# Gram matrices of a four-layer GNN kernel built from a symmetric W^T W: half the blocks on the high side, a one-sided product, and the transpose added by the tensor engine

## The chip, the core and the metric

The kernel runs on one core of one Trainium2 chip. The metric is the device time of one execution in microseconds, as the median over runs. The core has a tensor engine (PE, matmuls; its weight loads are shown as PEld), a vector engine (DVE), a scalar engine (ACT), GpSimd (POOL) and a sync engine (SP) that issues the DMAs. Each engine works through its own queue in order and waits on semaphores for the others.

## The reference, cut to what matters

Four graph layers follow each other on x of 32 batches x 256 nodes x 512 features, each with a residual and a layer norm. Layers 1 and 3 hold the Gram matrices:

```python
z_l = jnp.einsum('bnd,ed->bne', h, W_lang)
z_g = jnp.einsum('bnd,ed->bne', h, W_grav)
zn = z_l / jnp.maximum(jnp.linalg.norm(z_l, axis=-1, keepdims=True), EPS)
A_l = jnp.maximum(jnp.einsum('bnd,bmd->bnm', zn, zn), 0.0) * not_eye
sq = jnp.sum(z_g * z_g, axis=-1, keepdims=True)
d2 = jnp.maximum(sq + jnp.swapaxes(sq, -1, -2) - 2.0 * jnp.einsum('bnd,bmd->bnm', z_g, z_g), 0.0)
A_g = jnp.exp(-d2 / (2.0 * sigma * sigma)) * not_eye
...
out = jnp.einsum('bnm,bmd->bnd', K, v)
return jnp.einsum('bnd,ed->bne', out, W_O)
```

So each of the two layers needs, per batch, the two 256 x 256 matrices G = H^T (W^T W) H for W = W_lang and W = W_grav, where H is the layer's input, features by nodes. From G come the norms (its diagonal), the cosines and the distances. Layer 0 is an attention over features with a 256 x 256 mixing matrix, and layer 2 is a product with a fixed 256 x 256 matrix.

## The kernel before

Every value that goes through a matmul is held as a high part (the value rounded by ACT to the matmul's 32-bit format) and a low part (the rest, by DVE), and a product is the sum of three: high x high, high x low, low x high. DVE's subtraction for a low part is always line L809, ACT's rounding is L592.

The batches run in two streams, s = 0 and s = 1, with buffers of their own. The order of the work on each engine is written out by hand as a sequence of *slots*. In each slot one stream does the projections, Gram matrices and values of one layer (1 or 3), while the other stream's remaining steps are put between them. A turn takes two batches (one of each stream) through all layers in four slots: middle, middle, seam, seam. There are 16 turns, 15 of them in full in a loop, and a start ahead of them in which the weights are prepared.

- A **middle slot** mixes in, for the other stream: norm_rows (the transposed norms, L311), transpose_k, mix_values (out = K v), layer2, and transpose_x (the next layer's input turned around).
- A **seam slot** mixes in the end of layer 3 of one batch of the other stream and layer 0 of its next batch: adj_x, k_rows, aggregate (L371, L375), softmax_sums (L384), sum_rows, transpose_x.

The steps of the slot's own stream, on PE, are: `project` (z = W h, 48 matmuls of 128x256 for each of W_lang and W_grav: L419 and L420 with the high part of h, L425 with its low part), `gram` (G = z^T z, 24 matmuls of 128x256 for each of the two, L441) and `values` (v, 24 matmuls of 128x512, L303 and L307). L303 and L307 are the helper `product`, L311 is the helper `flip`, a transpose on PE of a 128 x 128 block.

On DVE, `split_z` takes the low part of z. `squares_l` (L964) and `gauss_start` (L979) read the diagonals of the two Gram matrices, `norm_squares` (L988) writes the norms out as a matrix whose transposes norm_rows makes, and `cosine_start` is L972. `kernel_rows` and `kernel_mix` (L997 to L1022) build K. `scale_agg` is L935 and `normalise` L879; L1031 is add_kv, L1042 add_bias2, L927 and L928 sum_squares. POOL does an inverse square root for each norm (L1203, L1207), one split per batch (L1190) and the attention sums (L1199).

In the start, `prepare` flips the weights W_lang, W_grav and W_O block by block and splits them into high and low; the products W_O W_V ("vo") are made by matmuls. The eight weight matrices go through two staging buffers, so a load waits until the buffer has been read.

Of the kernel before, what the change touches and what calls it, by code (L numbers as in the profile page):

```python
# [43 lines left out]
def gnn_stack(nc, x, adj, wq, wk, bm, w1l, w1g, w1v, w1o, gate1, sigma1, bias2,  # L44
# [9 lines left out]
    with ctx:  # L54
# [86 lines left out]
        def squares(row):  # L141
# [39 lines left out]
        gram_done = sems("gram_done")  # L181
        v_done = sems("v_done")
# [31 lines left out]
        wv_rounded = sem("wv_rounded")  # L214
        wv_split = sem("wv_split")
# [8 lines left out]
        jobs = [("l", 0), ("o", 0), ("vo", 0), ("g", 0), ("l", 1), ("o", 1), ("vo", 1), ("g", 1)]  # L224
        nat_a, nat_b = full[1][:, 0:4, :], full[1][:, 4:8, :]
        nat = {"l": nat_a, "o": nat_a, "g": nat_b}

        loads = [(w1l, nat_a, None, 0), (w1v, nat_b, None, 0), (w1o, nat_a, prep_pe, 4), (w1g, nat_b, wv_split, 2),
                 (w3l, nat_a, prep_pe, 8), (w3v, nat_b, prep_pe, 16), (w3o, nat_a, prep_pe, 20),
                 (w3g, nat_b, wv_split, 4)]  # L230
        load_of_job = {0: 0, 1: 2, 3: 3, 4: 4, 5: 6, 7: 7}
        load_of_wv = (1, 5)
        wv_hi, wv_lo = XS[1], VS[1]
        hi_of = {(k, l): w_hi[l][k] for l in range(2) for k in names}
        lo_of = {(k, l): w_lo[l][k] for l in range(2) for k in names}
        for l in range(2):
            hi_of["o", l], lo_of["o", l] = ZS[1][:, 0:4, :], ZS[1][:, 4:8, :]
        adj_nat = full[0][:, 2, :].rearrange("p (t m) -> p t m", m=nodes)
# [8 lines left out]
        def _(sp):  # L247
# [30 lines left out]
            sp.wait_ge(prep_pe, 24)  # L278
# [14 lines left out]
        def _(pe):  # L293
# [28 lines left out]
            def prepare(q):  # L322
                kind, l = jobs[q]
                if kind == "vo":
                    pe.wait_ge(prep_out, 4 * q)
                    pe.wait_ge(wv_split, 2 * l + 2)
                else:
                    pe.wait_ge(w_loaded[load_of_job[q]], 16)
                for t in range(FT):
                    dst = psum[1][:, t, :]  # L330
                    if q:
                        pe.wait_ge(prep_out, 4 * (q - 1) + t + 1)
                    elif t == 3:
                        pe.wait_ge(adj_prep, 1)
                    cols = slice(t * P, (t + 1) * P)
                    if kind == "vo":
                        last = product(dst, [(wv_hi[:, e, cols], wv_lo[:, e, cols],
                                              hi_of["o", l][:, e, :], lo_of["o", l][:, e, :]) for e in range(FT)])
                    else:
                        for e in range(FT):  # L340
                            last = flip(dst[:, e * P:(e + 1) * P], nat[kind][:, e, cols])
                    last.then_inc(prep_pe, 1)

# [64 lines left out]
            def project(s, j, l, kind, e):  # L408

                bank = (3, 0, 1, 2)[2 * kind + e // 2]  # L410
                dst = psum[s][:, bank, (e % 2) * nodes:(e % 2 + 1) * nodes]
                wh, wl = w_hi[l]["lg"[kind]], w_lo[l]["lg"[kind]]
                cols = slice(e * P, (e + 1) * P)
                first = kind == 0 and e == 0
                for h in range(2):
                    if first:
                        pe.wait_ge(hth_ready[s], j * 4 + (2 * l + h + 1))
                    for d in (2 * h, 2 * h + 1):
                        mm(dst, wh[:, d, cols], HTH[s][:, d, :], start=(d == 0), stop=False)  # L419
                        mm(dst, wl[:, d, cols], HTH[s][:, d, :], start=False, stop=False)  # L420
                for h in range(2):
                    if first:
                        pe.wait_ge(htl_ready[s], j * 4 + (2 * l + h + 1))
                    for d in (2 * h, 2 * h + 1):
                        last = mm(dst, wh[:, d, cols], HTL[s][:, d, :], start=False, stop=(d == FT - 1))  # L425
                if e % 2:
                    last.then_inc(z_done[s], 1)

            def gram(s, j, l, kind, n):

                if n == 0:
                    pe.wait_ge(zl_ready[s], j * 8 + (4 * l + 2 * kind + 1))
                    pe.wait_ge(zh_ready[s], j * 8 + (4 * l + 2 * kind + 2))
                zh, zl = ZH[s][kind], ZL[s][kind]
                cols = slice(n * P, (n + 1) * P)
                hi = [(zh[:, e, cols], zh[:, e, :]) for e in range(FT)]
                lo = [p for e in range(FT) for p in ((zh[:, e, cols], zl[:, e, :]), (zl[:, e, cols], zh[:, e, :]))]
                for i, (a, b) in enumerate(hi + lo):
                    if n == 0 and i == len(hi):
                        pe.wait_ge(zl_ready[s], j * 8 + (4 * l + 2 * kind + 2))  # L440
                    last = mm(psum[s][:, (3, 1)[kind], n * nodes:(n + 1) * nodes], a, b,  # L441
                              start=(i == 0), stop=(i == 3 * FT - 1))
                if n == NT - 1:
                    last.then_inc(gram_done[s], 1)

            def values(s, j, l, n):

                cols = slice(n * P, (n + 1) * P)
                wh, wl = w_hi[l]["vo"], w_lo[l]["vo"]
                product(psum[s][:, 2 * n, :],  # L450
                        [(HTH[s][:, d, cols], HTL[s][:, d, cols], wh[:, d, :], wl[:, d, :])
                         for d in range(FT)]).then_inc(v_done[s], 1)
# [43 lines left out]
            def start():  # L496

                prepare(0)
                pe.wait_ge(adj_prep, 1)
                adj_x(0, 0)  # L500
                prepare(1)
                k_rows(0, 0)
                prepare(2)
                prepare(3)
                prepare(4)
                aggregate(0, 0, (0, 1, 2, 3))
                prepare(5)
                softmax_sums(0, 0)
                sum_rows(0, 0)
                prepare(6)  # L510
                prepare(7)
                transpose_x(0, 0, 0)

            def middle_slot(s, js, l, r, jr):

                norm_rows(r, jr, 0)
                for e in range(FT):
                    project(s, js, l, 0, e)
                transpose_k(r, jr, 0)
                project(s, js, l, 1, 0)  # L520
                mix_values(r, jr, 0)
                for e in range(1, FT):
                    project(s, js, l, 1, e)
                gram(s, js, l, 0, 0)
                gram(s, js, l, 0, 1)
                layer2(r, jr)
                gram(s, js, l, 1, 0)
                gram(s, js, l, 1, 1)
                values(s, js, l, 0)
                transpose_x(r, jr, 1)  # L530
                values(s, js, l, 1)

            def seam_slot(s, js, l, r, jr, jn):
# [3 lines left out]
                for e in range(3):  # L537
                    project(s, js, l, 0, e)
# [4 lines left out]
                project(s, js, l, 0, 3)  # L543
                project(s, js, l, 1, 0)
# [4 lines left out]
                project(s, js, l, 1, 1)  # L549
                if jr is not None:  # L550
                    mix_values(r, jr, 1, jn)
                project(s, js, l, 1, 2)
                project(s, js, l, 1, 3)
                if jn is not None:
                    aggregate(r, jn, (0, 1), jr)
                gram(s, js, l, 0, 0)
# [3 lines left out]
                gram(s, js, l, 0, 1)  # L560
                if jn is not None:
                    sum_rows(r, jn)
                gram(s, js, l, 1, 0)
                gram(s, js, l, 1, 1)
                values(s, js, l, 0)
                values(s, js, l, 1)
# [23 lines left out]
        def _(act):  # L590
# [3 lines left out]

            def prepare(q, tiles=range(FT)):
                for t in tiles:
                    act.wait_ge(prep_pe, 4 * q + t + 1)
                    run(hi_of[jobs[q]][:, t, :], psum[1][:, t, :]).then_inc(prep_hi, 1)

            def round_wv(l):  # L600
                act.wait_ge(w_loaded[load_of_wv[l]], 16)
                for h in range(2):
                    run(wv_hi[:, 2 * h:2 * h + 2, :], nat_b[:, 2 * h:2 * h + 2, :]).then_inc(wv_rounded, 1)
# [66 lines left out]

            def split_v(s, j, l, n):
# [39 lines left out]
            def start():  # L711
                split_x(0, 0)
                prepare(0)
                round_wv(0)
                split_adj_x(0, 0)
                prepare(1)
                gates()
                softmax_columns(0, 0)
                attention_start(0, 0)
                prepare(2, (0, 1))  # L720
                attention_end(0, 0)
                prepare(2, (2, 3))
                prepare(3)
                prepare(4)
                round_wv(1)
                prepare(5)
                sum_row(0, 0)
                relu_rows(0, 0)
                prepare(6)
# [3 lines left out]
            def middle_slot(s, js, l, r, jr):  # L733
# [3 lines left out]
                split_z(s, js, l, 0, 1)  # L737
                split_kt(r, jr, 0)
                split_z(s, js, l, 1, 0)
                split_x2(r, jr)  # L740
                split_z(s, js, l, 1, 1)
# [4 lines left out]
            def seam_slot(s, js, l, r, jr, jn):  # L746
# [9 lines left out]
                split_z(s, js, l, 0, 1)  # L756
                if jn is not None:
                    softmax_columns(r, jn)
# [4 lines left out]
                split_z(s, js, l, 1, 0)  # L763
                if jn is not None:
                    attention_end(r, jn)
                split_z(s, js, l, 1, 1)
# [28 lines left out]
        def _(dve):  # L795
# [53 lines left out]
            def prepare(q, tiles=range(FT)):  # L849
# [421 lines left out]
```

## Time and profile before

| | us |
|---|---|
| median of 3 runs | 2265.52 (2262.24 to 2265.63) |
| the profiled execution: its own time | 2265.96 |
| the profiled execution: span, first to last instruction | 2264.2 |
| PE busy in the span | 2230.2 (98%) |
| DVE busy | 1814.6 (80%) |
| ACT busy | 811.3 (36%) |
| POOL busy | 376.7 (17%) |
| one full turn of four slots | 136.8 |

A time of the device is about 1.8 us above the span of the same execution. The busy share of an engine is an average over slots with different limits; which wait ends last in a slot has to be read from the timeline of that slot. Slot boundaries are told by norm_rows, the first four flips of a slot.

### The profile page before, as it was taken

Reading aid. Unit: us, or ns where it says so; the run is one execution under the profiler, and the core shown is the slowest. Engines: PE = TensorE matmul, PEld = TensorE weight load, DVE = VectorE, ACT = ScalarE, POOL = GpSimd, SP = SyncE. Lnnn points to the kernel's source line nnn. Section 1 sums busy time; section 2 is a strip of 40 time slices with the busy share of each in tenths; the row PEclk is TensorE's granted clock in tenths of the full one; section 3 lists DMA queues with packets and bytes.
Section 4 is the critical chain, followed back from the end, with each engine's and each line's share of the span. In section 5 each row is a group of like instructions: output and inputs, shape, how many; then the busy total and the mean of one; then the engine's idle time right before and its main releaser. Section 6 shows DMA issues by size and latency. Waiting matters only on the chain.

```text
span 2264.2 us, 37798 instructions
## 1 busy us (share of the span) xinstructions
PE 2230.2 (98%) x15204; PEld 2046.7 (90%) x15204; DVE 1814.6 (80%) x4601; ACT 811.3 (36%) x1513; POOL 376.7 (17%) x326
## 2 busy tenths in 40 slices
PE   7999999999999999999999999999999999999997
PEld 5899999989999899999989999899999999999896
DVE  7678788787887878878787887878888787887875
ACT  5424234242433424333242333424334242342421
POOL 1102121120211202112120211202112021211200
PEclk9999999999999999999999999999999999999998
DMA  5000000000000100000000000100001000000000
GB/s 177 19 1 11 29 10 29 1 29 10 10 29 1 38 1 10 29 10 29 1 10 29 10 29 1 38 1 10 29 1 38 1 11 29 10 29 1 20 1 19
DMA packets 23664, 44.89 MB, mean 20 GB/s; under 512 B 2625, under 2 KB 2881, under 8 KB 23489
## 3 DMA queue, kind: packets, MB, share of 16 engines
q1 hardware_dynamic: 23488, 42.48, 5.6%
q8 instruction: 120, 1.97, 0.4%
q14 instruction: 56, 0.45, 0.1%
HBM read 25.70 MB, written 16.78 MB: 19 GB/s over the span
## 4 chain that ended last, share of the span: by engine, by line
PE 84%; DVE 12%; issue 3%; ACT 1%; DMA 0%; POOL 0%; SPq 0%; POOLq 0%; DVEq 0%; ACTq 0%
PE psum L303 20%; PE psum L441 14%; PE psum L307 10%; PE psum L425 10%; PE psum L419 10%; PE psum L420 9%; PE psum L311 6%; DVE zs L809 5%; DVE full L917 2%; PE psum L375 2%; DVE stats L865 2%; PE psum L371 1%; PE psum L384 1%; ACT vs L592 1%; DVE full L1031 1%
## 5 line engine op out<-in xcount | busy, mean ns | idle before, releaser
L441 PE MATMUL psum<-zs 128*128 128x256 f32 x3072 | 398.6, 285 | 0.0
L441 PEld LDWEIGHTS psum<-zs 128*128 128x128 f32 x3072 | 382.8, 192 | 4.9
L592 ACT ACTIVATE zs<-psum 128x512 fp32r<-128x512 f32 (+1 forms) x456 | 238.7, 532 | 397.0 <-PE psum L425 305.6
L1203 POOL TENSOR_TENSOR rstd<-veps,minus_half 128x2 f32<-128x2 f32 x128 | 102.2, 798 | 1207.9 <-DVE veps L874 1207.9
L809 DVE TENSOR_TENSOR zs<-psum,zs 128x512 fp32r<-128x512 f32 (+1 forms) x456 | 266.9, 610 | 23.5 <-ACT zs L592 21.7
L592 ACT ACTIVATE vs<-psum 128x512 fp32r<-128x512 f32 x128 | 76.5, 598 | 553.8 <-PE psum L307 553.8
L1199 POOL TENSOR_TENSOR full<-full 128x512 f32<-128x512 f32 x96 | 145.5, 1516 | 442.3 <-DVE zs L809 433.8
L311 PE MATMUL psum<-ident,full 128*128 128x128 f32 x1412 | 191.6, 276 | 19.1 <-DVE full L1022 5.2
L311 PEld LDWEIGHTS psum<-ident,full 128*128 128x128 f32 x1412 | 165.0, 142 | 34.6 <-DVE full L1022 5.5
L865 DVE BATCH_NORM_STATS2 stats<-full 128x6 f32<-128x512 f32 x256 | 163.5, 681 | 0.0
L1031 DVE SCALAR_TENSOR_TENSOR full<-psum,rdeg,full 128x512 f32<-128x512 f32 x128 | 96.0, 750 | 82.6 <-PE psum L307 82.6
L879 DVE TENSOR_SCALAR full<-full,mv,rstd 128x512 f32<-128x512 f32 x256 | 128.1, 542 | 35.0 <-POOL rstd L1203 35.0
L809 DVE TENSOR_TENSOR zs<-full,vs 128x512 fp32r<-128x512 f32 x128 | 148.9, 1203 | 1.3
L303 PE MATMUL psum<-vs,zs 128*128 128x512 f32 x512 | 139.6, 394 | 0.7 <-ACT zs L592 0.7
L371 PE MATMUL psum<-vs,zs 128*128 128x512 f32 x512 | 139.3, 394 | 0.8 <-ACT vs L592 0.8
L419 PE MATMUL psum<-xs,w0l_hi 128*128 128x256 f32 x512 | 131.6, 290 | 0.3 <-ACT xs L592 0.3
L419 PE MATMUL psum<-xs,w1g_hi 128*128 128x256 f32 x512 | 130.6, 288 | 0.0
L419 PE MATMUL psum<-xs,w1l_hi 128*128 128x256 f32 x512 | 130.6, 288 | 0.0
L419 PE MATMUL psum<-xs,w0g_hi 128*128 128x256 f32 x512 | 130.6, 288 | 0.0
L809 DVE TENSOR_TENSOR vs<-psum,vs 128x512 fp32r<-128x512 f32 x128 | 87.9, 687 | 52.3 <-ACT vs L592 52.3
L303 PE MATMUL psum<-w0vo_hi,xs 128*128 128x512 f32 x512 | 129.4, 395 | 0.0
L303 PE MATMUL psum<-w1vo_hi,xs 128*128 128x512 f32 x512 | 128.9, 394 | 0.0
(139 smaller groups left out, 5097.1 us busy)
## 6 DMA issues: line engine op xcount, KB each, us to landing
full<-in_x_dram SPq DMA_DIRECT2D x32, 512.0 KB, 4.1
out_dram<-full SPq DMA_DIRECT2D x32, 512.0 KB, 2.9
full<-in_L_gnn_W_lang_dram SPq DMA_DIRECT2D x2, 1024.0 KB, 6.2
full<-in_L_gnn_W_V_dram SPq DMA_DIRECT2D x2, 1024.0 KB, 7.1
full<-in_L_gnn_W_O_dram SPq DMA_DIRECT2D x2, 1024.0 KB, 6.6
full<-in_L_gnn_W_grav_dram SPq DMA_DIRECT2D x2, 1024.0 KB, 5.7
full<-in_adj_dram SPq DMA_DIRECT2D x1, 256.0 KB, 2.6
bias_row<-in_L_gnn_bias_dram SPq DMA_DIRECT2D x1, 256.0 KB, 6.9
```

The source lines that it names most:

```text
L303: mm(dst, a, b, start=(n == 0), stop=False)
L307: ins = mm(dst, a, b, start=False, stop=(n == len(last) - 1))
L311: return mm(dst, src, ident[:], is_transpose=True, start=True, stop=True)
L371: mm(psum[s][:, bank, :], y[s][:, t, o * P:(o + 1) * P], ATH[s][t], start=(t == 0 and y is YTH), stop=False)
L419: mm(dst, wh[:, d, cols], HTH[s][:, d, :], start=(d == 0), stop=False)
L420: mm(dst, wl[:, d, cols], HTH[s][:, d, :], start=False, stop=False)
L425: last = mm(dst, wh[:, d, cols], HTL[s][:, d, :], start=False, stop=(d == FT - 1))
L441: last = mm(psum[s][:, (3, 1)[kind], n * nodes:(n + 1) * nodes], a, b, start=(i == 0), stop=(i == 3 * FT - 1))
L592: return nc.scalar.activation(dst, src, func, **kw)
L809: return tt(dst, src, plain(hi), ALU.subtract)
L865: ins = nc.vector.bn_stats(stats[s][:, n, :], CUR[s][:, n, :])
L1199: nc.gpsimd.tensor_tensor(ATT[s][0], ATT[s][0], ATT[s][t], ALU.add).then_inc(att_sum[s], 1)
```

## The change

The Gram matrix is built from S = W^T W. In the start, S is made once for each of the four matrices: the weight is split as it lies (no flips), and `prepare` multiplies it with itself, only the blocks on and above the diagonal (widths 512, 384, 256 and 128). `mirror` flips these blocks for the part below. The low buffer of S holds the low parts on and above the diagonal; its diagonal blocks are low parts of *half* the block, and the high parts of the halved diagonal blocks lie in the unused part below.

In a slot, `project_hi` multiplies the high part of h with the upper triangle T of S alone (diagonal halved, S = T + T^T), so 20 matmuls for each kind instead of 32; `project_lo` multiplies the low part of h with the whole high part of S (16, as before). `gram` multiplies the result, high and low, with the high part of h: 16 matmuls for each kind instead of 24. ACT copies this half Gram matrix to memory (`copy_gram`), and `symmetrise` flips it on PE in four blocks that are added to the same bank. `values` is cut into head and tail, which are put at different places. DVE's readers of the diagonals now wait for `sym_done`. All other work is the same, except for its order.

```diff
-        jobs = [("l", 0), ("o", 0), ("vo", 0), ("g", 0), ("l", 1), ("o", 1), ("vo", 1), ("g", 1)]
+        jobs = [("l", 0), ("g", 0), ("o", 0), ("vo", 0), ("l", 1), ("g", 1), ("o", 1), ("vo", 1)]
...
+                    else:
+                        hi, lo, rest = part_hi[kind], part_lo[kind], slice(t * P, U)
+                        last = product(dst[:, rest], [(hi[:, e, cols], lo[:, e, cols], hi[:, e, rest], lo[:, e, rest])
+                                                      for e in range(FT)])
...
+            def project_hi(s, j, l, kind, es):
+                wh, wl = w_hi[l]["lg"[kind]], w_lo[l]["lg"[kind]]
+                for e in es:
+                    cols = slice(e * P, (e + 1) * P)
+                    for d in range(e + 1):
+                        if kind == 0 and d == e and e % 2 == 0:
+                            pe.wait_ge(hth_ready[s], j * 4 + (2 * l + e // 2 + 1))
+                        top = diag_hi(wl, d) if d == e else wh[:, d, cols]
+                        mm(project_bank(s, kind, e), top, HTH[s][:, d, :], start=(d == 0 and e % 2 == 0), stop=False)
+                        mm(project_bank(s, kind, e), wl[:, d, cols], HTH[s][:, d, :], start=False, stop=False)
...
+            def symmetrise(s, j, l, kind):
+                pe.wait_ge(gram_copied[s], j * 4 + (2 * l + kind + 1))
+                bank, half = halves(psum[s][:, (3, 1)[kind], :]), halves(M[s][:, (1, 3)[kind], :])
+                for n in range(NT):
+                    for m in range(NT):
+                        last = mm(bank[:, n, m * P:(m + 1) * P], half[:, m, n * P:(n + 1) * P], ident[:],
+                                  is_transpose=True, start=False, stop=(n == NT - 1 and m == NT - 1),
+                                  skip_group_check=True)
+                last.then_inc(sym_done[s], 1)
...
             def seam_slot(s, js, l, r, jr, jn):
...
-                gram(s, js, l, 0, 0)
+                gram(s, js, l, 0)
                 if jn is not None:
                     aggregate(r, jn, (2, 3))
                     softmax_sums(r, jn)
-                gram(s, js, l, 0, 1)
+                gram(s, js, l, 1)
+                symmetrise(s, js, l, 0)
+                values_head(s, l, 0)
                 if jn is not None:
                     sum_rows(r, jn)
-                gram(s, js, l, 1, 0)
-                gram(s, js, l, 1, 1)
-                values(s, js, l, 0)
-                values(s, js, l, 1)
+                symmetrise(s, js, l, 1)
+                values_tail(s, l, 0)
+                values_head(s, l, 1)
+                values_tail(s, l, 1)
                 if jn is not None:
                     transpose_x(r, jn, 0)
...
+            def copy_gram(s, j, l, kind):
+                act.wait_ge(gram_done[s], j * 4 + (2 * l + kind + 1))
+                run(M[s][:, (1, 3)[kind], :], psum[s][:, (3, 1)[kind], :]).then_inc(gram_copied[s], 1)
```

The first place is PE's queue in a seam slot, from the sums of the softmax (ones,full1) to the flips that wait for smat_ready1, which are sum_rows. Before:

```order
L384 MATMUL psum1<-ones,full1 128x1 [waits att_sum1]
L384 MATMUL psum1<-ones,full1 128x1 x3
L441 MATMUL psum0<-zs0 128x256 x12
L311 MATMUL psum1<-ident,full1 128x128 [waits smat_ready1]
L311 MATMUL psum1<-ident,full1 128x128 x3
```

And now (L481 is gram, L492 symmetrise, L505 and L506 the eight matmuls of values_head, L330 flip):

```order
L420 MATMUL psum1<-ones,full1 128x1 [waits att_sum1]
L420 MATMUL psum1<-ones,full1 128x1 x3
L481 MATMUL psum0<-xs0,zs0 128x256 [waits zh_ready0,zl_ready0]
L481 MATMUL psum0<-xs0,zs0 128x256 x11
L481 MATMUL psum0<-xs0,zs0 128x256 [waits zl_ready0]
L481 MATMUL psum0<-xs0,zs0 128x256 x3
L492 MATMUL psum0<-ident,full0 128x128 [waits gram_copied0]
L492 MATMUL psum0<-ident,full0 128x128 x3
L505 MATMUL psum0<-w0vo_hi,xs0 128x512
...
L506 MATMUL psum0<-w0vo_lo,xs0 128x512
L330 MATMUL psum1<-ident,full1 128x128 [waits smat_ready1]
L330 MATMUL psum1<-ident,full1 128x128 x3
```

Between the sums and sum_rows stood 12 matmuls of 128x256; now 16 of them, four flips and eight matmuls of 128x512 stand there.

The second place is PE's queue in a middle slot, from the end of layer2 (xs0,w2_hi) to norm_rows (the flips that wait for mat_ready1). Before:

```order
L307 MATMUL psum0<-xs0,w2_hi 128x512 x2
L441 MATMUL psum1<-zs1 128x256 [waits zh_ready1,zl_ready1]
L441 MATMUL psum1<-zs1 128x256 x3
L441 MATMUL psum1<-zs1 128x256 [waits zl_ready1]
L441 MATMUL psum1<-zs1 128x256 x19
L303 MATMUL psum1<-w0vo_hi,xs1 128x512 x8
L307 MATMUL psum1<-w0vo_lo,xs1 128x512 x4
L311 MATMUL psum0<-ident,full0 128x128 [waits cur_ready0]
```

And now (L511 is values_tail):

```order
L326 MATMUL psum0<-xs0,w2_hi 128x512 x2
L492 MATMUL psum1<-ident,full1 128x128 [waits gram_copied1]
L492 MATMUL psum1<-ident,full1 128x128 x3
L511 MATMUL psum1<-w0vo_hi,xs1 128x512 x4
L505 MATMUL psum1<-w0vo_hi,xs1 128x512
...
L506 MATMUL psum1<-w0vo_lo,xs1 128x512
L330 MATMUL psum0<-ident,full0 128x128 [waits cur_ready0]
```

The 24 Gram matmuls that stood behind layer2 have moved ahead of it, and four flips stand in their place; values(0) is 12 matmuls behind layer2 in both, four as the tail of the first half and eight as the head of the second.

## Rows read from the trace of the kernel before

**Rows 1.** The page: span, busy time, the chain's shares by engine

```profile
span 2264.2 us, 37798 instructions
...
PE 2230.2 (98%) x15204; PEld 2046.7 (90%) x15204; DVE 1814.6 (80%) x4601; ACT 811.3 (36%) x1513; POOL 376.7 (17%) x326
...
PE 84%; DVE 12%; issue 3%; ACT 1%; DMA 0%; POOL 0%; SPq 0%; POOLq 0%; DVEq 0%; ACTq 0%
```

**Rows 2.** Busy time by stretch: one turn, middle, seam, seam, middle slot

```profile
core 0: us, PE busy (x) PEld busy (x) DVE busy (x) ACT busy (x) POOL busy (x), PEclk, DMA share, GB/s
273.53:303.50 29.97, 29.97 (x210) 27.91 (x209) 21.70 (x60) 7.46 (x14) 2.07 (x3) 1.00 0.01 1
303.50:341.86 38.36, 38.28 (x266) 35.03 (x263) 33.08 (x80) 17.21 (x33) 9.68 (x7) 1.00 0.04 15
341.86:380.24 38.38, 38.30 (x263) 34.92 (x261) 33.69 (x82) 17.19 (x34) 9.70 (x7) 1.00 0.13 42
380.24:410.30 30.06, 30.06 (x208) 27.84 (x207) 22.90 (x62) 7.39 (x15) 2.07 (x3) 1.00 0.00 1
```

**Rows 3.** The chain of waits in a middle slot: start, length, what

```profile
281.59 0.93 PE psum L303 x4
...
288.65 2.88 PE psum L441 x24
...
297.15 1.84 PE psum L303 x8
298.99 0.91 PE psum L307 x4
299.90 0.87 PE psum L311 x8
```

**Rows 4.** The chain of waits in a seam slot

```profile
314.03 0.98 PE psum L311 x9
316.45 0.93 PE psum L303 x4
```

**Rows 5.** Timeline of a seam slot: DVE, and PE's sum_rows

```profile
304.79 0.75 DVE L997 TENSOR_TENSOR full<-psum,full 128x256 f32<-128x256 f32 x2
...
306.37 1.75 DVE L1013 SCALAR_TENSOR_TENSOR full<-full,adj_off 128x256 f32<-128x256 f32 x1
...
317.87 0.75 DVE L1031 SCALAR_TENSOR_TENSOR full<-psum,rdeg,full 128x512 f32<-128x512 f32 x1 [0.51 <-PE psum L307]
...
330.47 0.18 DVE L927 RECIPROCAL rsum<-psum 128x4 f32<-128x4 f32 x1
...
331.81 0.60 PE L311 MATMUL psum<-ident,full 128*128 128x128 f32 x4
...
333.08 1.29 DVE L935 TENSOR_TENSOR full<-psum,full 128x512 f32<-128x512 f32 x2 [1.96 <-ACT full L592]
...
338.75 1.00 DVE L879 TENSOR_SCALAR full<-full,mv,rstd 128x512 f32<-128x512 f32 x2
...
340.60 0.69 DVE L972 SCALAR_TENSOR_TENSOR full<-psum,adj_off 128x512 f32<-128x512 f32 x1
```

**Rows 6.** Timeline of a middle slot's end: DVE and POOL

```profile
294.31 0.69 DVE L1042 TENSOR_TENSOR full<-psum,bias_row 128x512 f32<-128x512 f32 x1 [0.67 <-PE psum L307]
...
297.54 1.00 DVE L879 TENSOR_SCALAR full<-full,mv,rstd 128x512 f32<-128x512 f32 x2 [0.80 <-POOL rstd L1203]
...
299.51 0.69 POOL L1207 TENSOR_TENSOR rnq<-sq_l,minus_half 128x2 f32<-128x2 f32 x1 [2.01 <-DVE gbias L984]
```

**Rows 7.** Busy time and granted clock (PEclk) by stretch, in the start

```profile
16.00:19.20 3.20, 1.28 (x12) 1.08 (x11) 3.20 (x5) 0.69 (x2) 0.00 (x0) 1.00 0.48 184
51.00:53.80 2.80, 1.14 (x8) 1.01 (x9) 1.77 (x5) 0.45 (x2) 0.00 (x0) 0.97 0.97 372
53.80:57.20 3.40, 3.40 (x9) 2.61 (x9) 2.75 (x5) 1.69 (x3) 0.00 (x0) 0.52 0.02 5
57.20:60.60 3.40, 3.40 (x16) 2.78 (x15) 2.51 (x9) 0.60 (x1) 0.70 (x1) 1.00 0.49 154
```

**Rows 8.** Timeline of the start: a weight's split on DVE, the first projection

```profile
16.43 2.35 DVE L809 TENSOR_TENSOR vs<-full,xs 128x1024 fp32r<-128x1024 f32 x2
...
69.30 0.39 PE L419 MATMUL psum<-xs,w0l_hi 128*128 128x256 f32 x1 [0.30 <-ACT xs L592]
```

More of the change, by code:

```diff
@@ L406, in transpose_x, with project_bank @@
                     last.then_inc(ht_done[s], 1)
-            def project(s, j, l, kind, e):
-                bank = (3, 0, 1, 2)[2 * kind + e // 2]
-                dst = psum[s][:, bank, (e % 2) * nodes:(e % 2 + 1) * nodes]
+            def project_bank(s, kind, e):
+                return psum[s][:, (3, 0, 1, 2)[2 * kind + e // 2], (e % 2) * nodes:(e % 2 + 1) * nodes]
+            def project_hi(s, j, l, kind, es):
                 wh, wl = w_hi[l]["lg"[kind]], w_lo[l]["lg"[kind]]
[L413 to L444, printed above, removed]
@@ new lines, in project_lo @@
+            def project_lo(s, j, l, kind, es):
+                wh = w_hi[l]["lg"[kind]]
+                for e in es:
+                    cols = slice(e * P, (e + 1) * P)
+                    for d in range(FT):
+                        if kind == 0 and e == 0 and d % 2 == 0:
+                            pe.wait_ge(htl_ready[s], j * 4 + (2 * l + d // 2 + 1))
+                        last = mm(project_bank(s, kind, e), wh[:, d, cols], HTL[s][:, d, :], start=False,
+                                  stop=(e % 2 == 1 and d == FT - 1))
+                last.then_inc(z_done[s], 1)
@@ new lines, in gram @@
+            def gram(s, j, l, kind):
+                pe.wait_ge(zl_ready[s], j * 8 + (4 * l + 2 * kind + 1))
+                pe.wait_ge(zh_ready[s], j * 8 + (4 * l + 2 * kind + 2))
+                bank = psum[s][:, (3, 1)[kind], :]
+                for y in (ZH[s][kind], ZL[s][kind]):
+                    for e in range(FT):
+                        if y is ZL[s][kind] and e == 2:
+                            pe.wait_ge(zl_ready[s], j * 8 + (4 * l + 2 * kind + 2))
+                        for n in range(NT):
+                            last = mm(halves(bank)[:, n, :], y[:, e, n * P:(n + 1) * P], HTH[s][:, e, :],
+                                      start=(y is ZH[s][kind] and e == 0 and n == 0),
+                                      stop=(y is ZL[s][kind] and e == FT - 1 and n == NT - 1))
+                last.then_inc(gram_done[s], 1)
@@ L454, in norm_rows, with values_tail @@
+            def values_tail(s, l, n):
+                for i, (xh, xl, wh, wl) in enumerate(values_terms(s, l, n)):
+                    last = mm(psum[s][:, 2 * n, :], xl, wh, start=False, stop=(i == FT - 1))
+                last.then_inc(v_done[s], 1)
             def norm_rows(s, j, l):
@@ L1051, in start @@
                 softmax_row(0, 0)
+                split_weight(2)
+                prepare(2)
                 for t in (0, 2):
```

223 lines of the change are left out of this document (147 added, 76 removed).

## The prediction, made before the changed kernel ran

> **What bounds the kernel now.** I read the page first. PE is busy 98% of a span of 2264.2 us, DVE 80%, and the chain that ended last is 84% PE but also 12% DVE [rows 1]. So less PE work should shorten it, but not everywhere, and the busy time by slot says where. A turn is two middle slots of 30.0 us, with DVE busy 21.7 and 22.9, and two seam slots of 38.4 us, with DVE busy 33.1 and 33.7 [rows 2]. A seam slot has 5 us of DVE slack in all. The timeline of a seam slot shows how little of that is real. From add_kv at 317.87 to the reciprocal of the softmax sums at 330.47, 12.60 us, DVE, ACT and POOL hand work to each other, and PE follows. Then sum_rows starts on PE at 331.81, ACT copies it, DVE starts scale_agg at 333.08 and runs without a gap until norm_squares ends where L972 starts, at 340.60 [rows 5]. The next slot's first PE step, norm_rows, waits for that. From the start of sum_rows to there it is 8.79 us.
>
> I call the end of norm_squares E, and work out the time from one E to the next.
>
> **What PE loses and gains in a slot.** Removed are 24 projection and 16 Gram matmuls of 128x256. 24 of them take 2.88 us, 0.120 each [rows 3], so 40 are 4.80 us. Added are 8 flips, 0.87 us [rows 3]. Net -3.93 us a slot, and over 64 slots -251 us, if PE were the only bound. DVE's instructions in a slot are the same ones in another order. ACT gets two copies of 128x512, 1.2 us against 7.4 to 17.2 busy in 30 to 38 [rows 2]; each falls behind a Gram product and has the next Gram product (1.92 us) or values_head (1.84 us) as cover before its flips. If that cover were gone, PE would stand 0.7 us per copy.
>
> **Middle slot.** From E, PE does: 0.1 latency, norm_rows 0.44, 50 matmuls of 256 (20+8+8+6+8) 5.99, transpose_k 0.44, 22 more 2.64. mix_values then starts at E+9.6 and takes 2.74 (12 matmuls of 512, at 0.228 from rows 3). Two Gram products of 16 are 3.83, four flips 0.44, values_head 1.84: layer2 starts at E+18.5 and ends at E+21.2. Behind it DVE is late: add_bias2's second half starts with layer2's end, at 294.31; normalise starts 3.23 later; POOL's inverse norm starts at 299.51, 5.20 later, and takes 0.69 [rows 6]; norm_squares needs another 0.4. So the next E is 6.3 us behind layer2's end, E+27.5. PE has only 0.44+0.91+1.84+0.87+0.91 = 5.0 us of work for this stretch (before: 2.87 of Gram more), so it stands for about 1.4 us in two or three pieces. A middle slot gains 2.5 of the 3.9 us: **27.5 us**.
>
> **Seam slot.** PE from E: 0.1, norm_rows 0.44, 28 matmuls 3.36, a wait of 0.2 for DVE's cosines (kernel_rows now starts 2.4 us behind E, behind four splits and L972 of 0.6 each), adj_x 2.9 (24 matmuls), 22 matmuls 2.64, nine flips 0.98 [rows 4], 22 matmuls 2.64: mix_values starts at E+13.2, and add_kv follows 1.42 later (316.45 to 317.87) [rows 4, 5], at E+14.7. DVE's own path to there is E+2.4 plus 13.1 (304.79 to 317.87) plus one split of 0.6 that now stands ahead, less 1.4 of waits in it and less about 0.9 of the stall of L1013, which took 1.75 us beside POOL's split [rows 5]: E+13.8. So PE leads by little. From add_kv to sum_rows it was 13.94 us. Here 16 Gram matmuls, four flips and values_head (1.92+0.44+1.84 = 4.20) replace 12 matmuls (1.44), all ahead of sum_rows: 16.7. Then the 8.79. The slot is 14.7+16.7+8.8 = **40.1 us against 38.4**: a slot with 3.9 us less PE work becomes 1.8 us longer, because sum_rows comes later behind a chain that was already nearly the limit. What is queued behind it on DVE (squares_l, add_x, the norm, gauss_start, norm_squares) waits with scale_agg. DVE's idle piece there grows from 1.96 to about 4.7 us.
>
> **The clock.** After sum_rows PE has 0.44+0.44+0.91+1.84+0.91 = 4.5 us of work, but transpose_x needs the first half of normalise, which starts 6.94 us behind sum_rows and ends 0.5 later [rows 5]. So PE stands 3.0 us, does eight flips in two pieces, and waits for norm_squares. In the start of the kernel before, the granted clock fell to half after stretches in which PE still did 1.28 us of work in 3.20, or 1.14 in 2.80 [rows 7]. Here it does 0.9 in over 4. I expect the clock to fall from 2.4 to 1.2 GHz in nearly every seam slot, about when the next begins. The price, from rows at either clock: 9 matmuls against 16 in 3.40 us [rows 7], so some 1.6 us of PE work lost, and the first 13 us of the next slot are PE's. [...] In the middle slots PE stands only 1.4 us in pieces, and I take no drop.
>
> A turn is then 27.5 (middle, before it a middle) + 29.1 (middle behind a seam) + 40.1 + 41.7 = 138.4 against 136.8: +1.6, times 15 = +25 us. The two middles of the last turn give 56.6-60.0 = -3.4. The last seam slot has no new batch mixed in, and gains its 3.9. The first seam, after the start, has no kernel_rows and is bound by the attention chain, 0.
>
> **The start.** Removed are 64 flips, -7.0 us. Added are four products of 48 matmuls, 12 each of width 512 (0.228), 384 (between, 0.17), 256 (0.120) and 128 (at most a flip's 0.109, at least half of the 256; I take 0.07): 7.1 us each, 28.4; and 24 mirror flips, 2.6. Net +24. Each product also waits for its weight to be rounded (ACT, about 2 us) and split (2.35 us on DVE [rows 8]), which used to run beside flips. Against that stand PE's gaps in the first 69.3 us [rows 8], mostly waits for loads. Walking the queues I get the first slot 22 us later. Bounds +15 and +32.
>
> **Sum.** +22+25-3-4 = +40 us on the profiled execution, whose time 2265.96 lies 0.4 above the median of 2265.52: **2305 us**.
>
> **The rivals.**
> *No clock drop, the rest as above* (2255 us). A turn is 2 x 27.5 + 2 x 40.1 = 135.2, -1.6 a turn, -23; the last slots -9, the start +22. For it: the flips may count as work. Against: rows 7. This ends on the other side.
> *Seam slots break even* (2207 us), also faster. If PE's way to mix_values is shorter than I have it and DVE's is the limit, with the stall of L1013 gone wholly (E+13.1), a seam is 38.5: a turn of 132.0, -4.8 x 15 = -71, and -9, +22. No way is left by which DVE's chain (13.1+16.7+8.8) makes it shorter, unless sum_rows comes earlier than the order says.
> *PE is the bound after all* (2037 us): -251+22. For it: 98% busy. Against: it needs DVE, busy 111 us of a turn, to fit without waits into 121; and the 8.79 us behind sum_rows.
> *The clock falls in middle slots too* (2355 us): turns of 2 x 29.1 + 2 x 41.7 = 141.6, +73; -6, +22. It decides if 1.4 us of standing in pieces is enough.
>
> **How the numbers follow.** Chances: my case 0.50, no drop 0.20, clock drops everywhere 0.10, seams even 0.12, PE-bound 0.03, something else 0.05. Each case is uncertain by about 15 us (0.25 us a slot). A measurement tells 0.2% (4.5 us) from no change. My case, the everywhere case and a sixth of the no-drop case are slower; the no-drop case's other part is faster by two thirds; the even and PE-bound cases are faster. That gives 0.29 faster, 0.08 same, 0.63 slower. The range takes in the even case's middle and most of the everywhere case: 2207 to 2350; my case alone would be 2285 to 2325.
>
> **What would show it.** Right: middle slots of 27 to 29 us and seam slots of 40 to 42; DVE waiting 4 to 5 us for ACT ahead of scale_agg; PE waiting for normalise ahead of transpose_x; a granted clock below 1.00 in most turns; the first slot starting near 91 us. Wrong: a seam slot under 38 us, or sum_rows less than 16 us behind add_kv, would break the main step; a clock at 1.00 throughout breaks the second.

## The result and the profile after

The changed kernel takes **2325.82 us** (median of 4 runs, 2322.56 to 2332.12) beside 2265.08 for the kernel before on the same chip: the ratio is 1.027 [1.025, 1.030], slower. The forecast was 2305 us. The profiled execution took 2332.12 us, its span is 2330.3.

The page of the changed kernel, with its span, the engines' busy time and the chain's shares, against [rows 1]:

```profile
span 2330.3 us, 34215 instructions
...
PE 2119.1 (91%) x13308; PEld 1857.5 (80%) x13308; DVE 1804.3 (77%) x4621; ACT 913.4 (39%) x1677; POOL 376.1 (16%) x326
...
PE 65%; DVE 27%; issue 3%; ACT 2%; POOL 2%; DMA 0%; SPq 0%; DVEq 0%; POOLq 0%; ACTq 0%
```

PE is busy 111 us less (2230.2 to 2119.1, some of it now at half clock) and stands 211 us instead of 34. DVE's work is nearly the same, but its share of the chain went from 12% to 27%. That is the case that the prediction describes: work was taken from an engine, and the other engine's chain did not get shorter. The list of waits of the changed kernel (us in total, times, longest) names the two places:

```profile
PEld psum L330 <- DVE full L989: 150.6, 126, 3.3
DVE full L1045 <- ACT full L662: 147.1, 32, 4.7
...
PE psum L330 <- DVE full L989: 109.2, 63, 2.8
```

L989 is normalise and L330 the flips, here transpose_x; L1045 is scale_agg. The timeline of a seam slot of the changed kernel (start, length, engine, instruction, in brackets the idle time before it and what ended it), against [rows 5]. L1082 stands right behind norm_squares, so its start is E, and L1141 is add_kv:

```profile
1028.24 0.68 DVE L1082 SCALAR_TENSOR_TENSOR full<-psum,adj_off 128x512 f32<-128x512 f32 x1
...
1043.29 0.75 DVE L1141 SCALAR_TENSOR_TENSOR full<-psum,rdeg,full 128x512 f32<-128x512 f32 x1 [1.11 <-PE psum L326]
...
1055.89 0.18 DVE L1037 RECIPROCAL rsum<-psum 128x4 f32<-128x4 f32 x1 [0.70 <-PE psum L420]
...
1060.00 0.60 PE L330 MATMUL psum<-ident,full 128*128 128x128 f32 x4
...
1061.27 1.29 DVE L1045 TENSOR_TENSOR full<-psum,full 128x512 f32<-128x512 f32 x2 [4.73 <-ACT full L662]
...
1066.94 1.00 DVE L989 TENSOR_SCALAR full<-full,mv,rstd 128x512 f32<-128x512 f32 x2
...
1067.54 2.04 PE L330 MATMUL psum<-ident,full 128*128 128x128 f32 x12 [2.83 <-DVE full L989]
...
1068.79 0.68 DVE L1082 SCALAR_TENSOR_TENSOR full<-psum,adj_off 128x512 f32<-128x512 f32 x1
```

The reciprocals of the softmax sums are there at 1055.89, but sum_rows, which needs them, starts at 1060.00, 4.11 us later (1.34 before), since PE first does the second Gram product, four flips and values_head. DVE stands 4.73 us (1.96 before), and E, the end of norm_squares, comes 8.79 us behind sum_rows, as before. In this slot E goes from 1028.24 to 1068.79.

Read this way from E to E through the whole trace, a middle slot that no slower clock touches is 27.77 us and a seam slot 40.55 (one seam slot of the trace is 0.35 us longer, between add_kv and the reciprocals). In the later half of the kernel a turn is steadily 27.77 + 40.56 + 42.48 + 29.14 = 139.95 us (136.8 before). The longer slot of each kind is the one that begins with a granted clock below full. Busy time and granted clock (PEclk) of the changed kernel at such a place, in pieces of 3.4 us:

```profile
1063.40:1066.80 3.40, 1.31 (x6) 0.75 (x4) 3.26 (x14) 1.01 (x2) 0.60 (x1) 1.00 0.00 0
1066.80:1070.20 3.40, 2.59 (x16) 2.12 (x17) 3.40 (x8) 1.67 (x4) 1.05 (x2) 0.89 0.00 0
1070.20:1073.60 3.40, 3.40 (x21) 3.40 (x20) 3.37 (x9) 1.84 (x3) 2.39 (x1) 0.61 0.00 0
1073.60:1077.00 3.40, 3.40 (x30) 3.40 (x30) 3.26 (x13) 1.72 (x4) 0.00 (x0) 1.00 0.00 0
```

PE works 1.31 of 3.40 us, and then the clock falls to 1.2 GHz for a few us and PE gets through 21 matmuls where at full clock it is 30. In 28 of the 31 seam slots a fall begins near the slot's end or just behind it. In the later turns the first of the two begins while PE still stands in the wait, here at 1205.98, ahead of the flips, which started at 1206.74:

```profile
1202.57:1205.98 3.41, 1.34 (x6) 0.76 (x5) 3.27 (x14) 1.04 (x2) 0.58 (x1) 1.00 0.00 0
1205.98:1206.74 0.76, 0.00 (x1) 0.01 (x1) 0.76 (x3) 0.00 (x0) 0.58 (x2) 0.50 0.03 11
```

The mean clock of the span is 0.967 (0.033 x 2330 / 0.5 = 154 us at half).

The start: the first projection of the first slot stood at 69.30 [rows 8]. The changed kernel's timeline has it at 103.17, and PE's longer waits behind the first product (41.90 and 88.71 begin the vo products, 71.58 is the second g product):

```profile
41.90 2.07 PE L322 MATMUL psum<-zs,xs 128*128 128x512 f32 x4 [1.41 <-DVE zs L908]
...
71.58 1.19 PE L322 MATMUL psum<-xs 128*128 128x512 f32 x4 [2.32 <-DVE vs L908]
...
88.71 2.08 PE L322 MATMUL psum<-zs,xs 128*128 128x512 f32 x4 [4.57 <-DVE zs L908]
...
103.17 0.39 PE L456 MATMUL psum<-xs,w0l_lo 128*128 128x256 f32 x1 [0.30 <-ACT xs L662]
```

### The profile page after: what moved, and what is told of

The parts are those of the page before. It is cut to its first block, busy times and chain, and to the rows that moved or that the text cites. A ratio compares the mean times of both kernels' runs of the same rounds, so it can differ in the third digit from the quotient of the medians.

```text
span 2330.3 us, 34215 instructions
## 1 busy us (share of the span) xinstructions
PE 2119.1 (91%) x13308; PEld 1857.5 (80%) x13308; DVE 1804.3 (77%) x4621; ACT 913.4 (39%) x1677; POOL 376.1 (16%) x326
## 3 DMA queue, kind: packets, MB, share of 16 engines
q1 hardware_dynamic: 23488, 42.48, 5.4%
## 4 chain that ended last, share of the span: by engine, by line
PE 65%; DVE 27%; issue 3%; ACT 2%; POOL 2%; DMA 0%; SPq 0%; DVEq 0%; POOLq 0%; ACTq 0%
PE psum L322 11%; PE psum L467 10%; PE psum L481 8%; PE psum L456 7%; PE psum L457 7%; PE psum L330 7%; DVE zs L908 6%; PE psum L326 5%; DVE stats L975 5%; DVE full L1027 3%; PE psum L505 3%; PE psum L506 3%; DVE full L989 2%; DVE full L1052 2%; DVE full L1045 2%
## 5 line engine op out<-in xcount | busy, mean ns | idle before, releaser
L330 PE MATMUL psum<-ident,full 128*128 128x128 f32 x1348 | 225.6, 305 | 132.8 <-DVE full L989 109.2
L330 PEld LDWEIGHTS psum<-ident,full 128*128 128x128 f32 x1348 | 166.5, 154 | 196.4 <-DVE full L989 150.6
L908 DVE TENSOR_TENSOR zs<-psum,zs 128x512 fp32r<-128x512 f32 (+1 forms) x456 | 259.7, 608 | 74.5 <-ACT zs L662 74.2
L662 ACT ACTIVATE full<-psum 128x512 f32<-128x512 f32 (+1 forms) x224 | 119.6, 534 | 447.3 <-PE psum L481 359.8
L481 PE MATMUL psum<-xs,zs 128*128 128x256 f32 x2048 | 262.9, 284 | 0.0
L481 PEld LDWEIGHTS psum<-xs,zs 128*128 128x128 f32 x2048 | 255.9, 191 | 5.1
L989 DVE TENSOR_SCALAR full<-full,mv,rstd 128x512 f32<-128x512 f32 x256 | 128.0, 541 | 53.9 <-POOL rstd L1317 53.9
L1045 DVE TENSOR_TENSOR full<-psum,full 128x512 f32<-128x512 f32 x64 | 41.2, 686 | 147.1 <-ACT full L662 147.1
L407 PEld LDWEIGHTS psum<-vs,zs 128*128 128x128 f32 x512 | 91.3, 188 | 74.0 <-issue 40.5
L662 ACT ACTIVATE xs<-psum 128x512 fp32r<-128x512 f32 x128 | 71.4, 596 | 193.8 <-PE psum L330 193.8
L1141 DVE SCALAR_TENSOR_TENSOR full<-psum,rdeg,full 128x512 f32<-128x512 f32 x128 | 95.9, 749 | 61.2 <-PE psum L326 59.1
L662 ACT ACTIVATE full<-full,b_col 128x512 f32<-128x512 f32 x128 | 88.6, 716 | 63.2 <-POOL full L1313 60.2
L662 ACT ACTIVATE vs<-full 128x512 fp32r<-128x512 f32 x128 | 80.0, 631 | 76.8 <-DVE full L1027 75.8
L322 PEld LDWEIGHTS psum<-vs,zs 128*128 128x128 f32 x512 | 93.1, 191 | 17.4 <-ACT zs L662 1.1
```

What stands on the lines that cost most here:

```text
L322: mm(dst, a, b, start=(n == 0), stop=False)
L330: return mm(dst, src, ident[:], is_transpose=True, start=True, stop=True)
L407: mm(psum[s][:, bank, :], y[s][:, t, o * P:(o + 1) * P], ATH[s][t], start=(t == 0 and y is YTH), stop=False)
L481: last = mm(halves(bank)[:, n, :], y[:, e, n * P:(n + 1) * P], HTH[s][:, e, :], start=(y is ZH[s][kind] and e == 0 and n == 0), stop=(y is ...
L662: return nc.scalar.activation(dst, src, func, **kw)
L908: return tt(dst, src, plain(hi), ALU.subtract)
```

## Experiments

Theory A is the prediction's: a seam slot's length is DVE's chain, reciprocals, then sum_rows, then 8.8 us to E, so it counts when sum_rows starts; and PE's standing in it lowers the clock. Its rivals, whose letters B and C each expectation sets anew, are that DVE is simply full, that only the half clock costs, or that PE's own work sets the slot. Another question is the start.

**Run 1: sum_rows directly behind the second Gram product.** In PE's seam slot:

```
                 gram(s, js, l, 1)
-                symmetrise(s, js, l, 0)
-                values_head(s, l, 0)
                 if jn is not None:
                     sum_rows(r, jn)
+                symmetrise(s, js, l, 0)
+                values_head(s, l, 0)
                 symmetrise(s, js, l, 1)
```

> The changed kernel, with sum_rows put directly behind the second Gram product in seam slots, so 4 flips and 8 matmuls of 512 (0.44 + 1.84 = 2.28 us) now follow it instead of standing ahead of it. Theory A (the queue): a seam slot ends 8.8 us behind sum_rows, so seam slots fall from 40.55 to 38.3 us; PE then stands under 1 us ahead of transpose_x instead of 2.8, so the granted clock should hardly fall any more and the slots of 41.3 to 42.5 us and 29.1 us go too. A turn of 139.9 becomes 2 x 27.8 + 2 x 38.3 = 132.2, and the time about 2326 - 15.5 x 7.7 = 2207 us. Theory C (DVE is simply full in a seam slot, busy 33.7 us plus its stalls, wherever sum_rows stands): seam slots stay near 40 us and the time above 2300 us. Theory B (only the half clock costs, the slot itself is no longer): 2280 us or so, with seam slots of 40.5.

Measured: 2220.87 us (2219.33 to 2221.52), ratio to before 0.980 [0.979, 0.982]. Seam slots are 38.33 us throughout, middles 27.77, the mean clock 0.994. Four flips in another place, no instruction more or less, turn 2.7% slower into 2.0% faster. Theory A holds with its number for the slot: sum_rows is 2.3 us earlier, the seam slot is 2.2 us shorter than the 40.55 without a drop, and the drops go with PE's wait, now 0.59 instead of 2.83 us. (The time was forecast 14 us lower, at 2207: that took every turn at 139.9 us, and in the first half of the changed kernel's trace the drops cost less than that or were missing.)

```profile
1022.75 2.04 PE L330 MATMUL psum<-ident,full 128*128 128x128 f32 x12 [0.59 <-DVE full L989]
```

**Run 2: the order as in the changed kernel, PE kept at work.** Ahead of transpose_x in the seam slots:

```
+            def keep_busy(s, j):
+                pe.wait_ge(rrow_ready[s], j + 1)
+                w = w_hi[0]["vo"]
+                for n in range(11):
+                    mm(psum[s][:, 1, :], w[:, 0, 0:P], w[:, 0, :], start=True, stop=True)
...
                 if jn is not None:
+                    keep_busy(r, jn)
                     transpose_x(r, jn, 0)
```

> The changed kernel, with 11 extra matmuls of 128x512 (2.5 us, their result is overwritten by the flips that follow) where PE stands 2.8 us in a seam slot ahead of transpose_x. They fit into the gap, so they move nothing by themselves. Theory A: the clock stays at 2.4 GHz, all seam slots take 40.55 and all middle slots 27.8 us, a turn falls from 139.9 to 136.7, and the time by 15.5 x 3 = 45 us to about 2280 us: slower than before still, by the start and by nothing else. If the clock does not matter: 2326 us, unchanged. If the whole loss is the clock's: below 2265 us.

Measured: 2290.10 us (2289.77 to 2290.85), ratio 1.011 [1.010, 1.013]; seam slots 40.56 and middles 27.77 throughout, clock 0.994. 11 matmuls more in each seam slot make the kernel 35.7 us faster than the changed one (46 were expected). So that is the price of the clock here. What is left, 24 us above before, is not in the turns: without a drop a turn is 136.66 us, against 136.8 before. The 15.7 us of PE work saved in each turn bring nothing, since the seam slots gave back what the middles gained, and the start (first projection at 102.10 in this run, 69.30 before) makes the kernel slower.

**Run 3: the same lateness put into the kernel before.**

```
-                if jn is not None:
-                    sum_rows(r, jn)
                 gram(s, js, l, 1, 0)
                 gram(s, js, l, 1, 1)
+                if jn is not None:
+                    sum_rows(r, jn)
```

> The kernel before, with one edit: sum_rows behind the second Gram product instead of ahead of it, so 24 matmuls (2.88 us) later. No matmul is added or taken. Theory A: norm_squares ends 8.8 us behind sum_rows; before, PE had 9.2 us of work there, now 6.4, so a seam slot grows from 38.4 to about 40.8 us, +2.4 x 31 = +74 us, and the granted clock may fall once PE stands 2 us: 2340 to 2370 us. Theory C or B: PE does the same work in another order, and the time stays within 10 us of 2265.

Measured: 2335.55 us (2332.46 to 2341.4), ratio 1.031 [1.029, 1.033]. Seam slots are 42.0 and 40.57 (39.1 and 38.4 before), middles 28.54 and 29.98 (29.25 and 30.01 before): a turn of 141.1. The expectation had 2340 to 2370. With no one-sided product at all, the kernel before loses 70 us from where sum_rows stands. In the profiled execution the clock stayed up (mean 0.997, against 0.967 in the changed kernel), so the 67 us by which it is longer are the chain's alone, and the timeline has a reason to offer: PE has more work left in the slot, and its wait ahead of transpose_x is half as long. Two of the four executions had a mean of 0.992 and took 2338 and 2341 us; whether their clock fell behind this wait, no trace shows.

```profile
911.99 2.05 PE L311 MATMUL psum<-ident,full 128*128 128x128 f32 x12 [1.47 <-DVE full L879]
```

**Run 4: sum_rows still earlier, between the high and the low half of the second Gram product.**

```
-            def gram(s, j, l, kind):
+            def gram(s, j, l, kind, between=None):
...
                 for y in (ZH[s][kind], ZL[s][kind]):
+                    if between and y is ZL[s][kind]:
+                        between()
                     for e in range(FT):
...
-                gram(s, js, l, 1)
+                gram(s, js, l, 1, (lambda: sum_rows(r, jn)) if jn is not None else None)
                 symmetrise(s, js, l, 0)
                 values_head(s, l, 0)
-                if jn is not None:
-                    sum_rows(r, jn)
                 symmetrise(s, js, l, 1)
```

> The changed kernel, with sum_rows between the high and the low half of the second Gram product in seam slots: another 8 matmuls (0.96 us) earlier than directly behind it, 3.24 us earlier than in the changed kernel. It is just after its input is ready (0.65 us behind the sums). Theory A: seam slots of 37.3 us, a turn of 130.2, time about 2326 - 15.5 x 9.7 = 2176 us. Theory C: no difference from putting it directly behind the product. If PE has become the bound by then (33.6 us of work in a seam slot and about 1 us of waits inside), the gain stays below 1 us a slot.

Measured: 2233.80 us (2232.8 to 2235.25), ratio 0.986; seam slots 38.76, *longer* than the 38.33 of run 1. Theory A as I had put it missed (it had 37.3 and 2176 us). The timeline of run 4:

```profile
1019.18 0.18 DVE L1037 RECIPROCAL rsum<-psum 128x4 f32<-128x4 f32 x1 [0.71 <-PE psum L420]
...
1020.04 0.60 PE L330 MATMUL psum<-ident,full 128*128 128x128 f32 x4
...
1021.63 1.09 ACT L662 ACTIVATE full<-psum 128x512 f32<-128x512 f32 x2 [6.32 <-PE psum L483]
...
1022.76 1.29 DVE L1045 TENSOR_TENSOR full<-psum,full 128x512 f32<-128x512 f32 x2 [2.93 <-ACT full L662]
```

sum_rows did come early, 0.86 us behind the reciprocals (1.82 in run 1). But ACT has two copies in a row there, and the first in its queue is copy_gram(1), released by the end of the Gram product (L483), which the flips in its middle have put off by 0.44 us. sum_rows' own copy stands behind it. So scale_agg starts 3.58 us behind the reciprocals, against 3.14 in run 1: the 0.44 is the slot's 0.43.

**Run 5: run 4, and ACT's two copies in the other order.** In ACT's seam slot:

```
                 copy_gram(s, js, l, 0)
-                copy_gram(s, js, l, 1)
                 if jn is not None:
                     sum_row(r, jn)
+                copy_gram(s, js, l, 1)
+                if jn is not None:
                     relu_rows(r, jn)
```

> The changed kernel with sum_rows between the high and the low half of gram(1), as in the run before, and on ScalarE the copy of sum_rows' bank (sum_row) queued ahead of copy_gram(1) instead of behind it. Theory A (ScalarE's order): in the run before, sum_rows came 0.9 us behind the softmax reciprocals, but its copy stood behind copy_gram(1), which waits for the end of the whole Gram product, and scale_agg started 2.7 us behind sum_rows instead of 1.3. With the copies swapped scale_agg starts 1.3 us behind sum_rows and 2.2 behind the reciprocals (with sum_rows behind the whole product: 3.1), so a seam slot is 37.4 us (38.33 less 0.96), the middles stay at 27.77, the kernel takes about 2192 us. Theory B (the low half of the Gram product, now 0.95 us later, holds up PE's way to the end of the slot): a seam slot stays at 38.3 or more, 2220 to 2235 us.

Measured: 2188.93 us (2187.71 to 2191.0), ratio 0.967 [0.965, 0.968]; seam slots 37.30, middles 27.77, as theory A had it (37.4). The timeline of run 5:

```profile
1037.02 0.18 DVE L1038 RECIPROCAL rsum<-psum 128x4 f32<-128x4 f32 x1 [0.70 <-PE psum L420]
...
1037.88 0.60 PE L330 MATMUL psum<-ident,full 128*128 128x128 f32 x4
...
1038.52 0.60 ACT L662 ACTIVATE full<-psum 128x512 f32<-128x512 f32 x1 [5.36 <-PE psum L330]
1039.47 0.60 ACT L662 ACTIVATE full<-psum 128x512 f32<-128x512 f32 x1 [0.36 <-PE psum L483]
...
1039.15 1.29 DVE L1046 TENSOR_TENSOR full<-psum,full 128x512 f32<-128x512 f32 x2 [1.48 <-ACT full L662]
```

Now the first copy is released by the flips (L330), and scale_agg starts 2.13 us behind the reciprocals, 1.01 less than in run 1; the slot is 1.03 shorter. The two orders together, PE's and ACT's, took 3.25 us out of a seam slot.

**Run 6: less TensorE work in the start.** The four l and g products of the start keep the 4 terms high times high of 12 in each block row; the 8 terms with a low part are left out.

```
+                if light:
+                    for n, a in enumerate(terms):
+                        ins = mm(dst, a[0], a[2], start=(n == 0), stop=(n == len(terms) - 1))
+                    return ins
...
-                                                      for e in range(FT)])
+                                                      for e in range(FT)], light=True)
```

> The changed kernel with 4 of the 12 matmuls in each block row of the four l and g products of the start (high times high part only; the low terms are left out), so 16 of 48 matmuls a product. The output is not the reference's. 128 matmuls are gone; the four products took 10.6, 7.7, 7.5 and 9.2 us in the changed kernel, so two thirds of some 31 us at full clock, 20 us of TensorE work. Theory A (TensorE's work sets the start): the first projection comes at about 83 us instead of 103.2. Theory B (rounding and splitting of the weights on ScalarE and VectorE, and the loads, set it): TensorE waits longer instead, and the first projection comes at 92 us or later. The rest of the kernel stays as it is, slots of 27.8 to 42.5 us.

Measured, with a single run: 2310.1 us, the first projection at 84.4. Busy time of the start (from 8 us to the first projection), in this order in the kernel before, the changed kernel and run 6, each from its own table of windows. The kernel before:

```profile
8.00:69.30 61.30, 51.85 (x265) 43.24 (x266) 47.64 (x87) 32.96 (x62) 8.06 (x5) 0.92 0.43 150
```

The changed kernel:

```profile
8.00:103.17 95.17, 80.34 (x417) 69.47 (x418) 56.59 (x107) 44.32 (x98) 8.02 (x5) 0.91 0.29 96
```

Run 6:

```profile
8.00:84.40 76.40, 58.49 (x290) 49.97 (x290) 55.27 (x107) 43.84 (x98) 8.02 (x5) 0.91 0.36 121
```

The change put 28.5 us of busy time on PE there (51.85 to 80.34) and 5.4 us of standing (9.45 to 14.83): the 33.9 us. Not all of the busy time is added work: by the granted clock (0.92 and 0.91 of these stretches) 17 us of the start ran at half clock, against 10 us before, besides the first matmuls of both, which took twice their later time. Run 6 takes 21.9 of busy time away and gets 18.8 back, the standing grows by 3.1. So it is mostly PE's work that sets the start (theory A gave 83, B 92 or more); the standing that is left ends mostly at a weight that ACT or DVE has just rounded or split. The traces of runs 1, 2, 4 and 5, whose start is the changed kernel's, have the first projection at 101.4 to 102.1, so 1 to 2 us of such a difference is chance.

**Run 7: all that was found, and two places more.** Run 5 with these edits. PE and ACT in the middle slots:

```
-                values_head(s, l, 0)
+                values_head(s, l, 0, (0, 1))
                 layer2(r, jr)
+                values_head(s, l, 0, (2, 3))
...
                 copy_gram(s, js, l, 0)
-                copy_gram(s, js, l, 1)
                 split_x2(r, jr)
+                copy_gram(s, js, l, 1)
```

and in ACT's start, and likewise in DVE's:

```
                 split_weight(3)
+                split_weight(4)
                 gates()
                 prepare(4)
-                split_weight(4)
```

> The run e5 plus two edits. In the middle slots ScalarE's split_x2 stands ahead of copy_gram(1), and layer2 stands in the middle of values_head(0), four matmuls ahead of it and four behind. In the start the rounding and splitting of the second g weight stand directly behind those of the second l weight. If VectorE's chain from layer2 to norm_squares sets a middle slot (theory A), layer2 starts 0.9 us earlier and a middle slot is 26.85 us instead of 27.77; 32 of them, 30 us. If TensorE's own work sets it (theory B), it stays at 27.8. Start: TensorE's wait of 2.3 us ahead of the second g product goes, first projection at 101 instead of 103.2. Seam slots as in e5. With theory A in both, about 2160 us.

Measured: **2163.07 us** (2161.81 to 2164.25), ratio to before 0.955 [0.954, 0.957]. Middle slots are 27.05 and seams 37.30 us. The middles gained 0.72 of the 0.92 that PE's cut gives: layer2 starts 0.08 us behind the four matmuls ahead of it, probably held by VectorE's and ScalarE's halves of x2, which the timeline doesn't name. The first projection comes at 96.77, against 103.17 in the changed kernel and 101.38 in run 5, whose start is the changed kernel's. 2.3 us of that is the wait ahead of the second g product; much of the rest is clock, of which 6.8 us stood at half against 13.7 in run 5 and 17.1 in the changed kernel. The start's timeline in run 7 shows this product's first matmuls without the wait, and the flips at 37 us at full clock (2.35 us for the same 12 in the changed kernel):

```profile
37.25 1.50 PE L330 MATMUL psum<-ident,full 128*128 128x128 f32 x12 [1.96 <-ACT w0g_hi L665]
...
66.30 1.17 PE L322 MATMUL psum<-xs 128*128 128x512 f32 x4
```

Nothing was edited at the flips, and their full clock has nothing to do with this order: in run 5 the same 12 take 1.50 us too.

## Why the prediction was right, and where its sizes were off

*That the seam slot gets longer with less PE work, because sum_rows comes later.* Right, and shown from both sides: moved back alone it gives the time back (run 1), moved alone in the kernel before it costs 70 us (run 3). The terms, from the slot shown above: add_kv at E+15.05 (forecast 14.7), sum_rows 16.71 behind it (16.7), E 8.79 behind that (8.79), DVE's wait 4.73 (4.7). The slot without a drop is 40.55 instead of 40.1: add_kv came 0.35 later than forecast, and the forecast's own terms (14.7, 16.7 and 8.8) add up to 40.2.

*The middle slot at 27.5.* It is 27.77. DVE's chain behind layer2 sets its end, as forecast: run 7 moved layer2 forward and the slot followed.

*The clock.* Right that it falls and where: 29.14 (29.1 forecast) for the middle slot behind a seam, 42.48 (41.7) for the second seam, a turn of 139.95 (138.4). It did so behind 28 of the 31 seam slots, and one turn ran through at full clock (norm_squares' copy starts at 931.83, 972.37, 1000.14, 1027.90 and 1068.45, so slots of 40.54, 27.77, 27.76 and 40.55). Run 2 puts the whole of it at 35.7 us, where the forecast of 3.2 us in 15 turns had 48. The stretch at 1063 us is of the kind of [rows 7], and so is the 3.41 us before the fall at 1205.98, in which PE worked 1.34 us at matmuls of 128x512. The Trainium skill ("TensorE: Matmul & The Clock Gate", Part 1) tells of a kernel in which TensorE stood for short times between groups of matmuls, often enough for its clock to go up and down between the two levels. The trace agrees: one wait of 2.83 us near a slot's end brought a fall in 28 of 31 cases. The first rival's thought that the flips may count as work is not settled: in the changed kernel PE did flips alone from 1064.71 to 1069.34 and the clock fell at 1069.45, but other falls came ahead of the flips, and run 2 put other matmuls into the wait and no more flips. What decides between 2.83 us of waiting with a drop and the same with none, I have not found.

*The start.* The forecast of +22 us (bounds 15 and 32) is the term that was mis-sized; it measures +33.9. The step that failed is "against that stand PE's gaps": it was a net +24 of work less what gaps would take up. The gaps took up nothing, they got 5.4 us longer. In the changed kernel PE stands 3.9 us (of the 5.68, from 8 us on) ahead of the first product and 2.32 ahead of the fourth, but also 1.41 and 4.57 ahead of the vo products and 1.96 ahead of flips, and not at all ahead of the third. And the busy time grew by 28.5, not 24. Four products at 7.1 us were forecast; the two that ran at full clock took 7.7 and 7.5, the other two, in part at half clock, 10.6 (11.92 to 22.48) and 9.2. So 2 of the 4.5 us are matmuls priced too low, and most of the rest is clock.

*The sum.* Against the profiled execution's 2332.12 the forecast is 26 us short: 12 us for the start, and for the slots 22 us (0.27 in a middle and 0.46 in a seam slot, 15 turns) less 12 for the clock. That is 22 of the 26. The range was 2207 to 2350 and the first rival, no drop, was 2255; with the start and the slots as measured it would be 2290, as run 2 shows, and also slower than before. So the side was surer than the 0.63 given to it: the sizes of the start and of the slots, both too low, hid that. That the forecast came within 1% of the median owes something to the clock's price, which was 12 us too high and stood against these two.

*The rival "seams break even", 2207.* It said that no way is left to a shorter seam "unless sum_rows comes earlier than the order says". That is what runs 1 and 5 do. The change itself isn't worthless: with the two queues reordered, and ahead of run 7's further edits, a turn is 130.1 us (run 5), 6.7 less than before, of the 15.7 us of PE work that went. No run put sum_rows earlier in the kernel before, where it started 1.34 us behind the reciprocals (0.86 in run 5), so how much of the gain that kernel could have had too isn't shown.

## What to carry to other kernels

When work is taken off the busiest engine in a program written out by hand, look at what now stands between two halves of another engine's chain: find the last instruction that the chain needs from the lightened engine (here four flips), and count the matmuls that the change puts ahead of it. Then do the same in every queue that hands the result on; a copy that is ready early is worth nothing behind one that is late (run 4 against run 5). And count preparation done once at full price, with its waits: here 24 us of added work cost 33.9.

## What the runs showed of the hardware

11 matmuls of 128x512 whose result nobody reads, in each of 31 seam slots, made the kernel 1.5% faster (2325.82 to 2290.10); the granted clock, 0.967 over the changed kernel's span, was 0.994 over run 2's, and no longer fell behind the wait. In the later turns a drop cost 1.37 us in a middle slot (29.14 for 27.77) and 1.92 in a seam slot (42.48 for 40.56). In the profiled executions a wait of 2.83 us with flips behind it brought one behind 28 of 31 seam slots, and waits of 1.47 (run 3) and 0.59 us (run 1) brought none.
